# The second bias of the feed-forward block: added by POOL to the residual, instead of by PE in the accumulation

## The reference

```python
for l in range(LAYERS):                       # 3 layers
    Y = _msr(_layernorm(X, ln1_w[l], ln1_b[l]), WQ[l], WK[l], WV[l], WG[l], WO[l], gn_w[l], gn_b[l], D) + X
    Hn = _layernorm(Y, ln2_w[l], ln2_b[l])
    X = jax.nn.gelu(Hn @ ffn_w1[l] + ffn_b1[l], approximate=False) @ ffn_w2[l] + ffn_b2[l] + Y
```

## Time and profile before

| what | value |
|---|---|
| median of 3 runs (range) | 2427.72 us (2426.78 to 2428.72) |
| the profiled execution: time, span | 2428.14 us, 2426.3 us |
| busy share of PE, PEld, DVE, ACT, POOL | 92%, 80%, 78%, 65%, 73% |
| mean granted clock of TensorE | 0.978 |

### The profile page before, as it was taken

The page is one execution under the profiler, slowest core; times in us unless marked ns, Lnnn a source line. Parts: engine busy times, 40 slices in busy tenths (PEclk is TensorE's granted clock), DMA queues, the critical chain, the costliest instruction groups (busy, mean ns, idle before and its releaser), DMA issues.

```text
span 2426.3 us, 52865 instructions
## 1 busy us (share of the span) xinstructions
PE 2233.4 (92%) x18308; PEld 1950.1 (80%) x18309; DVE 1887.8 (78%) x5669; ACT 1580.5 (65%) x5066; POOL 1764.3 (73%) x1762
## 2 busy tenths in 40 slices
PE   1489999999999999999999999999999999986985
PEld 0368888888888888888888888888888888875874
DVE  5757878888787888888888888887878888766653
ACT  0256677776767676776776777767676777763653
POOL 5687777777777777777787777777777774333777
PEclk9789999999999999999999999999999999997997
DMA  3111111111111111111111111111111111002332
GB/s 122 28 45 34 24 41 28 40 29 41 27 40 28 36 32 37 33 35 37 26 43 26 42 27 40 29 41 27 37 30 37 33 28 55 2 8 75 101 103 69
DMA packets 63522, 98.11 MB, mean 40 GB/s; under 512 B 19108, under 2 KB 41126, under 8 KB 63152
## 3 DMA queue, kind: packets, MB, share of 16 engines
q0 software_dynamic: 33216, 67.44, 10.6%
q1 hardware_dynamic: 30064, 27.53, 4.1%
HBM read 76.63 MB, written 19.17 MB: 39 GB/s over the span
## 4 chain that ended last, share of the span: by engine, by line
PE 75%; POOL 9%; DVE 8%; issue 4%; ACT 3%; DMA 0%; DVEq 0%; POOLq 0%; SPq 0%
PE psum L1471 65%; PE psum L1492 7%; POOL both_grams L760 4%; PE psum L1545 3%; POOL gr L795 3%; POOL out L821 3%; DVE hid L1254 2%; ACT qm L885 1%; ACT qkT L883 1%; ACT xn L896 1%; DVE side_n L1205 1%; DVE qk L1233 0%; DVE hid L1230 0%; DVE qk L1229 0%; POOL rstd L771 0%
## 5 line engine op out<-in xcount | busy, mean ns | idle before, releaser
L760 POOL DMA_INDIRECT both_grams<-gram_table,idx_all x768 | 780.3, 1016 | 188.5 <-issue 183.0
L1471 PE MATMUL psum<-xT,lw 128*128 128x256 f32 x1920 | 481.8, 385 | 0.0
L795 POOL TENSOR_TENSOR gr<-ms,con 128x8 f32<-128x8 f32 x192 | 319.1, 1662 | 137.9 <-DVE ms L1259 133.1
L1471 PE MATMUL psum<-lw,hid 128*128 128x129 f32 x3072 | 391.0, 276 | 3.4 <-ACT hid L915 3.4
L1471 PEld LDWEIGHTS psum<-lw,hid 128*128 128x128 f32 x3072 | 370.9, 192 | 12.9 <-issue 5.6
L771 POOL TENSOR_TENSOR rstd<-ss,con 128x2 f32<-128x2 f32 x320 | 233.9, 733 | 195.1 <-ACT squares L859 192.7
L1471 PEld LDWEIGHTS psum<-xT,lw 128*128 128x128 f32 x1920 | 341.2, 192 | 32.5
L915 ACT ACTIVATE hid<-psum,par 128x256 f32<-128x256 f32 x768 | 307.1, 486 | 43.8 <-PE psum L1471 41.1
L1471 PE MATMUL psum<-lw,xT 128*128 128x256 f32 (+1 forms) x1536 | 287.9, 330 | 6.5 <-ACT xT L871 6.5
L871 ACT ACTIVATE xT<-psum,par 128x256 f32<-128x256 f32 x384 | 213.5, 560 | 119.8 <-PE psum L1492 118.8
L1471 PEld LDWEIGHTS psum<-lw,xT 128*128 128x128 f32 x1536 | 250.0, 192 | 33.0 <-ACT xT L871 7.2
(11 more groups left out here) (244 smaller groups left out, 4747.6 us busy)
## 6 DMA issues: line engine op xcount, KB each, us to landing
both_grams<-gram_table,idx_all POOLq DMA_INDIRECT x768
xb<-x SPq DMA_DIRECT2D x32, 256.0 KB, 3.3
idx_all<-routed_rows SPq DMA_DIRECT2D x20, 132.0 KB
er<-routed_rows SPq DMA_DIRECT2D x20, 132.0 KB
both_grams<-routed_rows SPq DMA_DIRECT2D x20, 132.0 KB
qm<-routed_rows SPq DMA_DIRECT2D x20, 132.0 KB
both_grams<-expert_w SPq DMA_DIRECT2D x8, 321.0 KB, 5.2
lw<-layer_w SPq DMA_DIRECT2D x1, 2503.5 KB, 11.9
```

Source lines behind the costliest of these rows:

```text
L760: pool.indirect_dma_start(grams[s][:, g, c, :], None, gram_table, bass.IndirectOffsetOnAxis(ap=idx_all[:, g, at:at + 1], axis=0))\
L795: pool.tensor_tensor(gr[s][:, c], ms[s][:, c], const("half")[:, 0:n], ALU.pow).then_inc(y_r[s], 1)
L1471: return pe.matmul(dst, lhsT, rhs, start=start, stop=stop)
```

## The change

PE's two bias products go, and with them DVE's making of `bias2` and `three_bf`. In their place POOL adds the float32 bias `ffn_b2` to both chunks of `Y1` in SBUF, one operation of 128 x 2 x 129 per pass. It stands in POOL's queue at 7.2 units after the start of the feed-forward part, waits until ACT has applied the norm to `Y1` (`n_out`), and raises a new semaphore `y1_b`, for which DVE waits before it writes `X`.

```diff
 AT = {
+    "pool bias": ((7.2, 7.2, 7.2), (7.2, 7.2, 7.2), (7.2, 7.2, 7.2), (7.2, 7.2, 7.2)),
     "pool rstd1": ((-145.21, 1.48, 0.25), (32.6, 0.79, 0.07), (-145.21, 1.48, 0.25), (32.6, 0.79, 0.07)),
...
             def feed(it, s, l, h):
                 yield at("pool rstd2", it, s, h, l)
                 norm_rstd(it, s, 2 * l, h)
+                yield at("pool bias", it, s, h, l)
+                pool.wait_ge(n_out[s][h], nth(it, NORMS, 2 * l + 1))
+                pool.tensor_tensor(Y1[s][:, CS[h], 0:WIDE], Y1[s][:, CS[h], 0:WIDE],
+                                   param("ffn_b2", l, WIDE).unsqueeze(1).to_broadcast([P, 2, WIDE]), ALU.add)\
+                    .then_inc(y1_b[s], 1)
...
-            split_bias2()
...
                 dve.wait_ge(ff_p[s], nth(k, 2, h))
-                dve.wait_ge(y1_s[s], nth(k, 2, h))
+                dve.wait_ge(y1_b[s], nth(k, 2, h))
                 dve.tensor_tensor(X[s][:, cs, 0:WIDE], wide(bank_a(s, h)), Y1[s][:, cs, 0:WIDE], ALU.add).then_inc(x_s[s], 1)
...
                     for i in range(2):
-                        mm(wide(a)[:, i, :], hid[s][:, h, f, chunk(i)], w2[:, f, :], f == 0 and i == 0, False)
-                for i in range(2):
-                    last = mm(wide(a)[:, i, :], three_bf[:, :], bias2[:, l * WIDE:(l + 1) * WIDE], False, i == 1)
+                        last = mm(wide(a)[:, i, :], hid[s][:, h, f, chunk(i)], w2[:, f, :], f == 0 and i == 0,
+                                  f == FB - 1 and i == 1)
                 last.then_inc(ff_p[s], 1)
```

More of the change, by code:

```diff
@@ L317, in tower_program @@
         Y1 = two(sb, "Y1", [P, CH, WIDE + 1])
[L318 to L322, removed]
         xn = two(sb, "xn", [P, CH, H])
@@ L470, in tower_program @@
         y1_s = two(sem, "attention_residual_ready")
+        y1_b = two(sem, "attention_residual_with_bias_ready")
         f_p = two(sem, "ffn_hidden_in_psum")
```

## The result

The changed kernel took 2503.91 us (median of 5 runs, 2501.28 to 2506.14) against 2427.72 us before (5 runs): a ratio of 1.0314, 95% interval 1.0302 to 1.0325. That is 76 us slower, where 13 us were forecast, and lies outside the range that was given.

The account below looks back on a forecast made before the run. PE's queue was taken to set the pace. From 2428.1 us, - 21.1 + 26 + 5 + 3 = + 13 gave 2441 us; forecast range 2433 to 2453 (0.42), 8 in 10 range 2411 to 2466.

Parts of the forecast that it names:

- The condition that was named last: Sign of being wrong: delays add up between places, so POOL's queue and not PE's sets the pace.
- PE's relief: In PE's queue, dropping the two bias products saves 0.11 us a pass, 21.1 us over 192 passes.
- PE's lead: Where PE waits for ACT anyway, the 0.11 us just gained is waited away: 5 us lost.
- POOL's addition: Each of 192 additions takes 0.72 us on POOL, 0.75 with the step to the next operation, 144 us in all.
- The new waits: POOL's wait before each addition and DVE's wait before `X` cost nothing themselves.
- The three places: First layer (1, 1), (1, 0), (0, 0): no cover, PE loses 0.75, 0.59, 0.40 us, 26 us over 15 pairs.
- The nine others: Remaining places of a pair: a POOL wait follows first or the operand is early, so they cost nothing.
- The 326 us of POOL's waits: POOL's true reserve: 192.7 us waiting for sums of squares and 133.1 for `ms`, over twice what is added.
- The lock: DVE operations with two SBUF inputs and POOL's SBUF reads exclude each other: 29 us of DVE's time, 3 us let through.
- the kept gain: Rival: PE's time is kept as losses partly come back or additions are cheaper, about 2413 us; chance 0.25.
- no difference: Rival: losses and gain nearly equal, time within 0.2%, 2423 to 2433 us; chance 0.18.
- The slower one: Rival: additions take 0.83 us and all 29 us of DVE's lost time reaches PE, up to 2473 us; chance 0.15.

Follow-up runs that it names:

- the run with the three: Changed kernel with POOL adding only at (0, 0), (1, 0) and (1, 1) of the first layer, PE at the other nine: 2461.91 us, ratio 1.0134.
- the control: Changed kernel with two additions a pair given back to PE, (0, 1) middle layer and (1, 0) last layer: 2494.65 us, ratio 1.0283.
- the long fill: Changed kernel with each POOL addition replaced by a 728-element fill of a spare tile, bias left out: 2493.09 us, ratio 1.0268.
- three places with additions: Changed kernel, POOL adding only at (1, 1) first, (0, 1) middle, (1, 0) last layer, at moved positions, PE elsewhere: 2433.27 us; two 364-element fills per addition instead: 2428.10.
- six covered places: Changed kernel with POOL adding at six places a pair, at moved positions with a wait behind each, PE at the other six: 2444.84 us, ratio 1.0069.
- the short: Changed kernel with each POOL addition replaced by a 364-element fill at the same twelve places, bias left out: 2441.72 us, ratio 1.0055.

## Why the prediction was wrong in size

- What bounds the kernel: right for before. The condition that was named last, delays that add up until POOL's queue sets the pace, came true in part (POOL 39% of the chain, PE 30%).
- PE's relief at 21.1 us: too high. The run without any bias, where nothing of POOL's is in the way, shows 14.6: PE's busy time fell by 17.7 and its idle time grew by 3.1. Beside the additions 16 were foreseen (5 of PE's lead being waited away), and 5.5 came.
- DVE's setup at 0: no run takes it apart.
- POOL's addition at 0.72 us: 0.697 median, 0.743 mean. Right. The estimate by the Trainium skill's price (GPSIMD Engine Reference, section 3.1), 0.56 us before dispatch, is below the shortest of the 192, 0.672.
- The new waits at nothing: right; POOL waited 0.8 us for `n_out` in the whole run.
- The three places: 26 us and the 5 of the lead were foreseen, 37 us were measured. Nearly right as a sum, single places off by up to 0.36 us in the run with the three. The waits of 0.33 and 0.16 that the prediction takes for PE's stand on rows of PEld; PE's own rows had none. In the rivals' sums the `gr` of (1, 0) keeps 0.08 us too much (0.56 and 0.78 should be 0.48 and 0.70), 1 us in all.
- **The nine others at nothing: this is the step that failed.** "At the others a wait of POOL follows first …, or the operand is early" was judged for each place as if the other eleven additions weren't there. They lost 50 us. Shown causes: a wait was spent twice, by two additions in one stretch (the last layer's (1, 1) with the first layer's (0, 0) of the next pair; (1, 1) of the middle with (0, 0) of the last layer), which the run with one addition of each double removed shows, 27 us with what else these two cost; and the addition at place (0, 1) of the middle layer makes DVE late without a delay in POOL's queue, which the control shows, 9 us together with the other place given back. How much of that is reading SBUF was not taken apart.
- The 326 us of POOL's waits as a reserve: they gave up 58, not 144. They end with results that come from PE and DVE, and these came later as well, so much of a wait moves along with the delay and isn't used up. This is read from the trace; no run isolates it.
- The lock: 3 us were let through, of 29 us of DVE's time. DVE's busy time grew by 50 us over the kernel without a bias (1882.1 to 1932.2), and by 14 with the long fill. The long fill, which reads nothing, is 10.8 us faster than the changed kernel, of which about 5 are its shorter time (5.7 us at the 0.88 above), and three places with additions are 5.2 slower than with fills; both include DVE's wait for the addition. So 3 was too low; by how much is open. The count took only DVE's operations with two SBUF inputs. The row at 1000.35 shows an operation with a constant held as well. The Trainium skill has this too (SBUF — State Buffer, "Who interferes with whom"): casts and `tensor_scalar` can enter a mode that takes the port pair shared with GpSimd for the whole instruction. The trace agrees for `onehot`, a `tensor_scalar`: 0.85 us beside the addition, 0.35 at this place in the control. For the cast it shows the gather as well as the addition.

Of the rivals, the kept gain and no difference are out. The slower one, up to 2473, had the wrong mechanism: of the 91 us the fill shows 80 without reading SBUF. What stays open: of the 90 us of span between the profiles of the kernel without a bias and the changed one, 63 are idle time of PE (196.0 to 259.2), which the seven places explain in the main; 27 are busy time (2215.7 to 2242.9) of the same 17924 records, and which of them last longer, and why, was not taken apart. Open too is why six covered places cost 17.6 us.

## What to carry to other kernels

A wait of an engine is cover only once, and only for what stands in the same stretch of its queue: put all the operations that are added into the queue before pricing any, and carry the lateness from one to the next until a wait has taken it up. A wait that ends with a result of an engine that you delay may move along with the delay, so don't count it as a reserve. And a place with a wait behind it can still cost time through another engine, as (0, 1) of the middle layer did through DVE. A half-size dummy at the same places is a cheap test of this: 0.36 us lost per us for the short, 0.88 for what the long one had more.

## What the runs showed that was not expected

Beside POOL's work a very small DVE operation can take a multiple of its length. In the run with the long fill the 2-element conversion starts while a gather of POOL's is still under way, and ends 0.03 us behind the end of the fill that follows it:

```profile
995.38 0.95 POOL L760 DMA_INDIRECT both_grams<-gram_table,idx_all  x1 [0.30 <-issue]
995.61 1.47 DVE L1353 TENSOR_SCALAR slot<-slot_f 128x2 uint32<-128x2 f32 x1
996.33 0.72 POOL L804 MEMSET spare<- 128x728 f32 x1
```

So by these rows a gather and an operation that only writes hold it as well, while those with two SBUF inputs kept their 488 ns (mean of L1253 there; 560 for the same line, L1251, beside the additions).
